# A vision tower's last expert stage: remainders moved into narrower slots, and two weight-split steps moved in an earlier stage

## The reference, cut to what matters

```python
h = tok(x, W)                                # (8, 1024, 128)
h = h + L0_attn(layernorm(h))                # 8 heads of 16, softmax over 1024
h = h + L0_ffn(layernorm(h))                 # experts chosen per image, top 2 of 8
h = h + L1_attn(layernorm(h))                # attention within blocks
h = h + L1_ffn(layernorm(h))                 # experts chosen per token, top 2 of 8

def L1_ffn(x, Wr, W1, b1, W2, b2):           # flat: 8192 tokens
    top_vals, top_idx = top_k(flat @ Wr, 2)
    gates = scatter(softmax(top_vals), top_idx)
    for e in range(8):
        hdn = gelu(flat @ W1[e] + b1[e])     # 128 -> 512
        y = hdn @ W2[e] + b2[e]              # 512 -> 128
        out = out + gates[:, e:e + 1] * y
```

## Time and profile before

| what | value |
| --- | --- |
| three runs | 1415.1, 1416.4, 1413.77 us (median 1415.1) |
| the profiled execution's own time | 1412.59 us |
| its span, first to last instruction | 1410.8 us |
| busy in the span | PE 1184.4, ACT 992.8, DVE 917.3, POOL 556.0 us |
| mean granted TensorE clock | 0.916 |
| attention, sequence experts | 0 to 608 us, 608 to 833 us |
| block attention, token experts, adding | 833 to 1098 us, 1098 to 1375 us, 1375 to 1411 us |

### The profile page before, as it was taken

How to read it: one execution, slowest core, us unless ns; L and a number is a source line. 1 busy time by engine, 2 the same in 40 slices (tenths; PEclk the granted TensorE clock), 3 DMA queues, 4 the chain that set the end, 5 groups by cost and what they waited for, 6 DMA issues and landing times. The chain is left out here.

```text
span 1410.8 us, 26930 instructions
## 1 busy us (share of the span) xinstructions
PE 1184.4 (84%) x9386; PEld 795.3 (56%) x9386; DVE 917.3 (65%) x2573; ACT 992.8 (70%) x1348; POOL 556.0 (39%) x538
## 2 busy tenths in 40 slices
PE   3499999999999999979898966888861799999940
PEld 2245444444444444558777755777761688888830
DVE  4255767777877776678687766888641466666625
ACT  0389889898989899869787855444410799999930
POOL 3413333333233332121011111478776177777660
PEclk9899999999999999989999987798955899999975
DMA  3645554554637282132226510011116377777609
GB/s 87 118 110 127 117 129 107 127 131 102 152 80 169 64 170 64 39 128 92 88 85 232 178 50 1 18 41 47 45 48 237 119 238 240 234 251 238 239 25 357
DMA packets 93162, 180.56 MB, mean 128 GB/s; under 512 B 15597, under 2 KB 64200, under 8 KB 84960
## 3 DMA queue, kind: packets, MB, share of 16 engines
q1 hardware_dynamic: 72832, 129.18, 33.1%
q0 software_dynamic: 17344, 42.68, 9.1%
q10 hardware_dynamic: 2848, 6.95, 1.7%
HBM read 116.96 MB, written 63.12 MB: 128 GB/s over the span
## 5 line engine op out<-in xcount | busy, mean ns | idle before, releaser
L787 ACT ACTIVATE a_probs<-a_psS 128x1024 f32<-128x1024 f32 x512 | 482.4, 1035 | 69.0 <-PE a_psS L874 57.5
L886 PE MATMUL a_psO<-a_probs,a_v 128*32 128x256 f32 x4096 | 277.4, 388 | 1.1 <-issue 0.7
L1295 DVE TENSOR_TENSOR f_g_lo<-f_g,f_g_hi 128x512 fp32r<-128x512 f32 x284 | 193.5, 688 | 117.7 <-ACT f_g L1202 116.5
L2039 POOL DMA_INDIRECT result<-f_out,f_idx x156 | 181.2, 1162 | 98.4 <-issue 58.5
L886 PEld LDWEIGHTS a_psO<-a_probs,a_v 128*32 128x32 f32 x4096 | 107.5, 109 | 133.9 <-issue 85.4
L1595 POOL DMA_INDIRECT queue<-all_row,all_idx x128 | 125.2, 978 | 38.0 <-issue 37.4
L1199 ACT ACTIVATE f_g_hi<-f_psH,all_w 128x512 fp32r<-128x512 f32 x156 | 109.3, 701 | 19.8 <-PE f_psH L72 18.6
L1202 ACT ACTIVATE f_g<-f_psH,all_w 128x512 f32<-128x512 f32 x156 | 109.2, 700 | 0.0
L874 PE MATMUL a_psS<-ag_qs,ag_ks 50*128 50x512 f32 x512 | 96.7, 454 | 9.6 <-DMA ag_qs<-a_gparts 7.1
L874 PE MATMUL a_psS<-a_qs,a_ks 50*128 50x512 f32 x512 | 95.1, 447 | 4.0 <-ACT a_probs L787 1.5
L465 POOL TENSOR_TENSOR ag_rs_f<-ag_veps_f,all_half 128x4 f32<-128x4 f32 x32 | 33.3, 1042 | 133.6 <-DVE ag_veps_f L135 133.6
(11 more groups left out here) (370 smaller groups left out, 2619.7 us busy)
## 6 DMA issues: line engine op xcount, KB each, us to landing
all_w<-experts SPq DMA_DIRECT2D x39, 1026.5 KB, 5.4
experts<-ag_split POOLq DMA_DIRECT2D x32, 512.0 KB, 4.2
f_rows<-queue SPq DMA_DIRECT2D x39, 260.0 KB
f_w<-experts SPq DMA_DIRECT2D x8, 1026.5 KB, 5.9
qparts<-a_parts SPq DMA_DIRECT2D x16, 512.0 KB, 3.6
kparts<-a_parts SPq DMA_DIRECT2D x14, 512.0 KB, 3.1
ag_qs<-experts SPq DMA_DIRECT2D x4, 1026.5 KB, 5.2
ag_ks<-experts SPq DMA_DIRECT2D x4, 1026.5 KB, 5.0
```

What stands on the lines that cost most here:

```text
L787: nc.scalar.activation(probs[u % NPR][:, :], psS[score_buffer(u)][:, :, :].rearrange("p a n -> p (a n)"), ACT.Exp).then_inc(exp_done, 1)
L886: last = nc.tensor.matmul(psO[32 * g:32 * g + 32, a * HALF:(a + 1) * HALF], v[par][:, 2 * hp + p, kt, :], probs[u % NPR][:, cols:cols + HA ...
L1295: nc.vector.tensor_tensor(g_lo[i][:, n, :], g[:, n, :], g_hi[i][:, n, :].bitcast(F32), ALU.subtract).then_inc(lo_done, 1)
L2039: pool.indirect_dma_start(result, bass.IndirectOffsetOnAxis(ap=idx[i][:, j:j + 1], axis=0), out[i][:, j, :], None, bounds_check=2 * B * S ...
```

## The change

Three things are changed.

1. *Token experts.* The plan counts full tiles only (`steps` becomes 511, 1023, ... instead of 0, 512, ...). Full tiles take the first slots; the eight remainders follow, largest first, ranked by a pairwise comparison. A slot has `cols(m)` groups of 128 rows: slots 0 to 32 have 4, slots 33 to 38 have 3, 3, 2, 2, 1, 1. All that a slot does (rows loaded, transposes, products, activations, low parts, output, sends) is done over `cols(m) * 128` columns.
2. *Plan.* The first 25 of the 39 slots are planned before `planned` is raised, the rest after it by `plan_rest`. One more 256-byte table (`lower`) is loaded by SP in block attention, and DVE multiplies the slot numbers by 512 once, ahead of the loop.
3. *Weight splits.* In the first seven batches they stand at bursts 25 and 31 instead of 0 and 30. In the sequence experts there is a second raw buffer (`f_raw`), POOL loads one job more at the start of the block, and from then on the load of job j + 2 follows the store of job j.

```diff
-    SPLIT = [{0: 0, 30: 1}] * (B - 1) + [{5: 0, 12: 1}]
+    SPLIT = [{25: 0, 31: 1}] * (B - 1) + [{5: 0, 12: 1}]
...
+    def raw_place(self, j):
+        if j < self.FIRST_JOBS:
+            return 0, j + 1
+        r, i = divmod(j - self.FIRST_JOBS, 2)
+        return i, r + 1 + (0 if i else self.FIRST_JOBS)
...
+            shared.load_raw(pool, shared.FIRST_JOBS + 1, ins)
...
                 shared.store_split(pool, j, experts)
-                if j + 1 < len(shared.JOBS):
-                    shared.load_raw(pool, j + 1, ins)
+                if j + 2 < len(shared.JOBS):
+                    shared.load_raw(pool, j + 2, ins)
...
-            product(nc, psH[n][:, :], hi, lo, x_hi[j % 2][:, :], x_lo[j % 2][:, :]).then_inc(h_ps, 1)
+            product(nc, psH[n][:, 0:wide(m)], hi, lo, x_hi[j % 2][:, 0:wide(m)], x_lo[j % 2][:, 0:wide(m)]).then_inc(h_ps, 1)
...
+                whole(0, SURE)
+                dve.drain()
+                numbers(0, SURE)
                 dve.drain()
                 dve.sem_inc(planned, 1)
...
             plan()
+            plan_rest()
+
+
+def slot_cols(s, full):
+
+    return TPC if s < full else -(-(TPC * (7 - (s - full))) // 8)
...
-                for j in range(TPC):
+                for j in range(cols(m)):
                     pool.indirect_dma_start(result, bass.IndirectOffsetOnAxis(ap=idx[i][:, j:j + 1], axis=0), out[i][:, j, :], None,
                                             bounds_check=2 * B * S - 1, oob_is_err=False).then_inc(sent[i], 16)
```

More of the change, by code:

```diff
@@ L173, in __init__ @@
         self.FIRST_JOBS = 2 * E
-        self.raw, self.split = c.sb("raw", [P, CH]), c.sb("split", [P, 2, CH], F32R)
-        self.raw_in, self.split_done = c.sem("raw_in"), c.sem("split_done")
+        self.raw, self.split = [c.sb("raw0", [P, CH])], c.sb("split", [P, 2, CH], F32R)
+        self.raw_in, self.split_done = [c.sem(f"raw_in{p}") for p in range(2)], c.sem("split_done")
         self.aw_sum = c.sb("aw_sum", [P, 1])
@@ L1232, in turn_x @@
                 pe.wait_ge(x_done, j)
-            for i in range(TPC):
+            for i in range(cols(m)):
                 last = nc.tensor.transpose(psX[:, i * P:(i + 1) * P], rows(m)[:, i, 0:D], ident[:, :])
@@ L1252, in second @@
             hi, lo = second_parts(m, n)
-            last = product(nc, psY[i][:, :], hi, lo, g_hi[i][:, n, :], g_lo[i][:, n, :], first=(n == 0), last=(n == NB - 1))
+            last = product(nc, psY[i][:, 0:wide(m)], hi, lo, g_hi[i][:, n, 0:wide(m)], g_lo[i][:, n, 0:wide(m)], first=(n == 0), last=(n == NB - 1))
             if n == NB - 1:
@@ L1544, in block_attention @@
         steps, number = c.sb("steps", [1, 1, M]), c.sb("number", [1, N])
+        left_f, last_row, last_e, order = (c.sb(n, [1, 1, E]) for n in ("left_f", "last_row", "last_e", "order"))
+        in_rows, from_row = c.sb("in_rows", [1, 1, E]), c.sb("from_row", [1, N])
+        beats, ties, lower = c.sb("beats", [1, 1, E, E]), c.sb("ties", [1, 1, E, E]), c.sb("lower", [1, E, E])
         pad = c.sb("pad", [P, TPC, ROW])
@@ new lines, in numbers, with plan_rest @@
+            def numbers(lo, hi):
+                s = slice(lo, hi)
+                nc.vector.tensor_copy(tile_row[:, s], row_f[:, s])
+                nc.vector.tensor_copy(tile_e[:, s], e_f[:, s])
+            def plan_rest():
+                s, n = slice(SURE, N), N - SURE
+                whole(SURE, N)
+                nc.vector.tensor_tensor(left_f[:, :, :], n_f[:, :, :], in_rows[:, :, :], ALU.subtract)
+                nc.vector.tensor_scalar(last_row[:, 0, :], in_rows[:, 0, :], -float(E * STRIDE), None, ALU.add)
+                nc.vector.tensor_scalar(last_e[:, 0, :], number[:, 0:E], -float(E), None, ALU.add)
+                dve.drain()
+                nc.vector.scalar_tensor_tensor(last_row[:, 0, :], number[:, 0:E], float(STRIDE), last_row[:, 0, :], ALU.mult, ALU.add)
+                nc.vector.tensor_scalar(row_f[:, s], row_f[:, s], float(E * STRIDE), None, ALU.min)
+                rank(nc, dve, order[:, :, :], beats[:, :, :, :], ties[:, :, :, :], left_f[:, :, :], lower[:, :, :])
+                nc.vector.tensor_scalar(done_f[:, s], number[:, s], ends[:, 0, E - 1:E], None, ALU.subtract)
+                dve.drain()
+                nc.vector.tensor_tensor(over[:, s, :], order[:, :, :].broadcast_to([1, n, E]), done_f[:, s].unsqueeze(2).broadcast_to([1, n, E]), ALU.is_equal)
+                dve.drain()
+                nc.vector.tensor_tensor(part[:, s, :], over[:, s, :], last_row[:, :, :].broadcast_to([1, n, E]), ALU.mult)
+                dve.drain()
+                nc.vector.tensor_reduce(done_f[:, s], part[:, s, :], AX, ALU.add)
+                nc.vector.tensor_tensor(over[:, s, :], over[:, s, :], last_e[:, :, :].broadcast_to([1, n, E]), ALU.mult)
+                dve.drain()
+                nc.vector.tensor_tensor(row_f[:, s], row_f[:, s], done_f[:, s], ALU.add)
+                nc.vector.tensor_reduce(part[:, s, 0], over[:, s, :], AX, ALU.add)
+                dve.drain()
+                nc.vector.tensor_tensor(e_f[:, s], e_f[:, s], part[:, s, 0], ALU.add)
+                dve.drain()
+                nc.vector.tensor_scalar(e_f[:, s], e_f[:, s], float(E - 1), None, ALU.min)
+                dve.drain()
+                numbers(SURE, N)
@@ L1998, in token_experts, with cols, sends @@
     NW = len(w)
-    assert NB == 4
+    FULL = 2 * B * S // CH
+    assert NB == 4 and E == 8 and N == FULL + E - 1
+    def cols(m):
+        return slot_cols(m, FULL)
+    def sends(i, m):
+        return 16 * sum(cols(k) for k in range(i, m, 2))
     with ExitStack() as ctx:
@@ L2018, in load_rows @@
                     sp.wait_ge(x_ps, m - 1)
[L2019 removed]
+                sp.dma_start(rows[m % 2][:, 0:cols(m), :], queue[bass.ds(first, cols(m) * P), :].rearrange("(p i) c -> p i c", p=P)).then_inc(rows_in[m % 2], 16)
             def load_parts(m):
@@ L2041, in _ @@
             for i in range(2):
-                pool.wait_ge(sent[i], len(range(i, N, 2)) * 16 * TPC)
+                pool.wait_ge(sent[i], sends(i, N))
         def w_wait(eng, m):
```

87 lines of the change are left out of this document (47 added, 40 removed).

## The result

Four runs of the changed kernel took 1372.5 to 1387.0 us, median 1377.4, against 1415.1 before: 0.974 of it, with a 95% interval of 0.969 to 0.980. The forecast was 1383 in a range of 1374 to 1394. The profiled execution is the quickest of the four (1372.5, span 1370.7). In a second set of runs the kernel before had a median of 1410.6 in 19 runs and the changed one 1377.7: 32.9 us, ratio 0.977 (0.971 to 0.984). So the two comparisons put the change at 33 and 38 us, where 32 were forecast.

What follows compares the result with a forecast made beforehand. PE was busiest in attention (547.1 of 608 us) and the token experts (255.0 of 277), with POOL bounding the latter's end. Terms of 9.5 + 3.5 + 19 = 32 us off the median 1415.1 gave 1383, range 1374 to 1394.

Steps and rivals of the forecast that it cites:

- Term 1: Attention: moved splits end batch 0's stand and later batches' delays at the embedding; -9.5 us, between -12 and -5.
- The rival with collisions at burst 31: Attention: DVE's collisions eat the later batches' gain and stores hide behind loads; 1391.5 us, chance 0.17.
- Term 2: Sequence experts: with a second raw buffer, splits no longer wait for the load behind the store; -3.5 us.
- The bound of 0: Sequence experts: the second raw buffer gains nothing if stores land as late as loads (medians 4.2 and 4.5).
- Term 3: Token experts' tail: narrower slots cut sends from 32 to 20, POOL still bounds; -19 us, bounds -23 and -14.
- PE's item steps: Token experts, PE's steps 32 to 38: 26.8 us with narrow slots, where today they take 41.3 us.
- the rival of short products that keep their price: Token experts: products cost 0.23 us at any width, the tail becomes PE's, -14; 1388 us, chance 0.13.
- The rival in which the clock falls: Token experts' short slots: PE idles more, runs at 1.2 GHz and ends 14 us after POOL; 1397 us, chance 0.03.
- Most of PE's gain is cover: Token experts' end: POOL's sends end at 1351, later than PE at 1341, so POOL bounds.
- an estimate of 0.14 us for a product of 128 columns: Token experts: by the skill's ratio 0.14 us instead of 0.11, 72 products 2 us more on PE, end still POOL's.
- Edits at nothing: `plan_rest` (6 us on DVE, hidden behind POOL's row sends), SP's extra table and the tile order were priced at nothing.
- the sum of 32: Whole kernel: 9.5 + 3.5 + 19 = 32 us off, giving 1383 from the median.

Runs made afterwards that it cites:

- e1: Kernel before with only the weight splits moved to bursts 25 and 31 in the first seven batches; median 1398.6 us in 10 runs, 0.992 of before.
- e10: Changed kernel with the seventh batch's splits at bursts 14 and 25 instead of 25 and 31; 1381.5 us in six runs, 0.978 of before.
- e8: Changed kernel with a second split buffer in the sequence experts; median 1376.4 us in six runs, 0.975 of before.
- e7: Changed kernel with three buffers instead of two for the weighted rows; median 1378.0 us in six runs, 0.977 of before.
- e9: Changed kernel with splits of the first seven batches at bursts 25 and 30, so only burst 0's pair moved; median 1384.3 us in four runs, 0.977 of before.
- e5: Changed kernel with PE, ACT and DVE on all 512 columns in every slot, sends still narrow; median 1388.0 us in four runs, 0.983 of before.
- e2: Kernel before with only the second raw buffer in the sequence experts; median 1410.3 us in 10 runs, 1.000 of before.
- e3: Kernel before with only the narrower slots and the two-part plan; median 1388.9 us in four runs, 0.984 of before.
- e11: Changed kernel with second split buffer, three weighted-row buffers and the seventh batch's splits at 14 and 25; 1377.3 us in six runs, 0.976 of before.

## Why the prediction was right, and where it was not

**Term 1, splits: -9.5 forecast, 12.0 us measured alone.** The mechanism held. Batch 0 gave 7.5 us between the two executions shown instead of 6.5, as its whole stand and the slow group went. The under-sized term is the later batches. I took 0.62 us, ACT's stand in batch 4, for undisturbed, and it was not: burst 7 of the six later batches took 2.59 (batch 4) to 3.67 us (batch 1) and takes 2.11 in all of them now. That is 5.9 us in sum where I had 3, and 0.5 of it in every batch is what my base hid. Batch 1's other excess, 1.3 us in its last two bursts, is not the splits': e1 and e10, with the new places, have it there too. The rival with collisions at burst 31 did not come: of the 2.1 us of cover 1.1 were left, and PE wrote `a_psA` without a wait. The collision came at a place that I had not looked at, the score search at the head of the last batch. It gives back 0.7 us by itself, and 1.9 and 3.4 us with the fall of the clock behind it in the changed kernel's two profiles (67.2 and 68.7 against 65.3).

**Term 2, raw buffer: -3.5 forecast, nothing measured.** This step failed: "The load's wait goes and the store's stays: 2.8 us come off DVE". The bound of 0, "if stores land as late as loads", is what happened, and the rows to see it were there. With one split buffer a cast must wait for pair, issue and landing of the job before: 1.2 + 0.3 + 4.2 by the earlier trace rows, 5.7 us with the median landing and 6.9 in the job shown, where an item takes 6.2. The store was as long a chain as the load; it was only hidden behind it. e8 shows it: with a second split buffer the block took 200.5 us, 4.1 us less than the shortest execution without one. That the second raw buffer is needed beside it is argued and not shown: a second split buffer with one raw buffer was not run.

**Term 3, slots: -19 forecast, 20.2 us in the profiled tail (60.9 to 40.7), 21.7 timed alone.** Right in mechanism and size. POOL's 20 sends took 26.3 us with their waits, 27.1 forecast. The last of them starts at 1329.8, not 1337, because 19.8 us instead of 13 had gone ahead of the tail. PE's item steps, forecast at 26.8 us, took 26.5 in e7, where DVE waits 4.7 us for sends, and 30.4 with two buffers. The product starts were right to 0.01 us, so the rival of short products that keep their price is out. The rival in which the clock falls came in part. In e9 and e10 PE's granted clock was 0.56 and 0.55 in its last 8 to 10 us (1.00 in the changed kernel's last 9), and adding began 43.1 and 41.5 us after item 31's output instead of 40.7; the forecast had priced it at 14 us. "Most of PE's gain is cover" is half of it: with wide compute (e5) 9.5 us of the 20 are lost, so narrow compute is worth that much on top of narrow sends, and 4.6 without them.

The Trainium skill (TensorE: Matmul & The Clock Gate, Back-to-back issue gap) led to an estimate of 0.14 us for a product of 128 columns. The trace differs: 0.11, and the measurement decides. The 128-column products are 48 (24 in each of slots 37 and 38), not the 72 that the forecast counted. The Trainium skill (SBUF — State Buffer, Who interferes with whom) has DVE wait for a GpSimd operation already under way; the trace agrees in so far as the cast beside POOL's addition took 1.17 us in the sixth batch and 0.80 in the seventh, and 1.36 in the kernel before, instead of 0.43, and ended 0.28 to 0.29 us after POOL's operation each time. In the earlier trace rows that operation is the one before the addition of the earlier trace rows, which the forecast put beside the pair; it ended at 466.0.

**Edits at nothing.** The plan's second part ended at 1053.5 us on DVE, the last row left POOL at 1070.4; block attention's own 3.2 us are the clock's. The 40.1 us between the two executions shown are thus the terms and some luck: that of before had a slow batch 1 (69.0 where e2 and e3 had 67.1 and 66.9) and a slow block attention. It is luck as well that the sum of 32 came so near to the 32.9 timed in the second set: two terms were too small by 2.5 and 2.7 us and one too large by 3.2. The 0.2% that I took for telling a change from none was too fine, with runs of one kernel up to 15 us apart; the ratios' intervals reach 0.3 to 0.7% to either side.

## What to carry to other kernels

When a transfer is the last to release an engine, work out the next chain to the same instruction before crediting the wait: here a load and a store of about equal length ended at the same cast, two buffers for the load alone gave nothing, and two for both gave the time. A tail in which one engine sends and another computes must be narrowed on both, and each half alone shows how far the other would go. Before calling a step "undisturbed", look for a place where it cannot be disturbed; the smallest of six disturbed ones is not a base.

## What the runs showed that I had not expected

- Behind a drain on POOL, work went on only when POOL's own transfers had landed: in e10 the next operation started 8.32 us late, 0.3 us after the load's landing at 10.3 us; in e11 the same place lost 7.56 us, 0.3 us after a landing of 9.6. In the changed kernel, with no transfer of POOL's under way there, the same two operations are 0.32 us apart. No run takes the drain away, so that it is the drain that waits is read from these times alone.
- Behind a stand of PE of 1.9 us instead of 1.19 its clock fell to 1.2 GHz in seven executions and stayed up in e1, and it also fell in e9 with PE busy throughout. Such falls come at places that change from run to run, and the last batch alone took 65.3 to 71.3 us. Whole runs fit that: of e8's six, the two with a mean granted clock of 0.919 took 1368.5 and 1369.5 us, the four at 0.906 and 0.907 took 1376.3 to 1381.0.
- POOL stands 4.6 us in the middle of one slot's sends, always behind the 113th with two buffers and not at all with three.
